# A decoder layer for Trainium2: stacked rows of the cross-attention scores laid 8 partitions apart, the queries' rounded parts sent from ScalarE's queue, and another merge order

## The reference

```
q = _w8a8_linear(x, wq, bq).reshape(B, N, H, D).transpose(0, 2, 1, 3)
k = (cond @ wk.T + bk).reshape(B, L, H, D).transpose(0, 2, 1, 3)
scores = jnp.einsum('bhnd,bhld->bhnl', q, k) * inv_sqrt_d + mask[:, None]
attn = jax.nn.softmax(scores, axis=-1)
```

## Time and profile before

| what | value |
|---|---|
| median of 3 runs | 423.77 us (422.56 to 424.12) |
| the profiled execution | 420.01 us, of which the span of the instructions is 418.2 us |
| PE busy | 365.5 us, 87% of the span |
| DVE busy | 293.8 us, 70% |
| ACT busy | 194.2 us, 46% |
| POOL busy | 149.2 us, 36% |
| TensorE's granted clock, mean | 0.935 of full speed |

### The profile page before, as it was taken

One profiled execution on the slowest core, in us unless ns is written; L12 is line 12 of the kernel. 1 busy time (PEld: TensorE's weight loads), 2 busy tenths in 40 slices (PEclk: granted clock), 3 DMA queues, 4 the chain that ended last, 5 costly groups with the idle time before them and its releaser, 6 DMA issues. The chain is left out here.

```text
span 418.2 us, 7505 instructions
## 1 busy us (share of the span) xinstructions
PE 365.5 (87%) x2526; PEld 309.2 (74%) x2526; DVE 293.8 (70%) x848; ACT 194.2 (46%) x352; POOL 149.2 (36%) x162
## 2 busy tenths in 40 slices
PE   8977879996899999997999999999998455887795
PEld 7646769884788888795898778979778435745684
DVE  3999957584687879965688479659857844775522
ACT  1573547152447664643738535456663020383230
POOL 5495738842633443424135234242223300000101
PEclk9998969998999999999999999999999955968889
DMA  8937134786523535765134247462222253000000
GB/s 295 353 104 262 52 126 151 220 163 148 103 102 96 160 103 150 118 145 117 53 104 125 77 152 114 101 115 79 79 63 102 44 69 39 16 2 2 0 27 25
DMA packets 29798, 45.55 MB, mean 109 GB/s; under 512 B 3648, under 2 KB 20544, under 8 KB 29760
## 3 DMA queue, kind: packets, MB, share of 16 engines
q1 hardware_dynamic: 28944, 44.28, 40.4%
q10 hardware_dynamic: 816, 0.79, 0.8%
HBM read 26.31 MB, written 5.24 MB: 75 GB/s over the span
## 5 line engine op out<-in xcount | busy, mean ns | idle before, releaser
L1426 POOL TENSOR_TENSOR q_T<-q_T,rope_s 128x512 f32<-128x512 f32 x24 | 30.7, 1284 | 74.0 <-DMA rope_s<-rope_t 72.1
L1242 DVE CUSTOM_DVE_ANT_0 q_int<-bank,mask_s 128x256 bf16<-128x256 f32 x128 | 45.2, 416 | 15.9 <-PE bank L698 15.7
L1437 POOL TENSOR_TENSOR a_lo<-a_flat,a_hi 128x512 fp32r<-128x512 f32 x32 | 41.4, 1296 | 38.2 <-ACT a_flat L875 38.2
L618 PE MATMUL acc<-wo_s,a_hi 128*128 128x256 f32 x256 | 49.9, 294 | 0.8 <-POOL a_lo L1437 0.8
L586 PE MATMUL bank<-v_s,p_near 128*128 128x129 f32 x256 | 42.9, 279 | 4.1 <-POOL p_near L1444 3.8
L586 PEld LDWEIGHTS bank<-v_s,p_near 128*128 128x128 f32 x256 | 37.1, 194 | 11.6 <-issue 9.5
L1461 POOL TENSOR_TENSOR small<-small,half 128x2 f32<-128x2 f32 (+1 forms) x16 | 10.5, 656 | 94.2 <-DVE small L1132 94.1
L618 PEld LDWEIGHTS acc<-wo_s,a_hi 128*128 128x128 f32 x256 | 40.3, 193 | 3.1 <-POOL a_lo L1437 1.4
L915 ACT ACTIVATE p_near<-bank 128x512 f32<-128x512 f32 x32 | 19.1, 596 | 48.2 <-PE bank L563 34.9
L513 PE MATMUL bank<-x_hi,wqkv_hi 128*128 128x256 f32 x124 | 39.2, 316 | 0.0
L563 PE MATMUL bank<-q_T,k_T 128*128 128x512 f32 x64 | 34.7, 627 | 1.9 <-POOL q_T L1426 1.9
(11 more groups left out here) (167 smaller groups left out, 953.8 us busy)
## 6 DMA issues: line engine op xcount, KB each, us to landing
wo_s<-wo_parts SPq DMA_DIRECT2D x24, 512.0 KB, 3.5
rope_s<-rope_t SPq DMA_DIRECT2D x54, 128.0 KB, 2.3
wo_parts<-wo_s SPq DMA_DIRECT2D x8, 512.0 KB, 3.1
kS<-xo_T SPq DMA_DIRECT2D x24, 128.0 KB, 4.6
qS<-xo_T SPq DMA_DIRECT2D x24, 128.0 KB, 4.3
xs<-in_wo SPq DMA_DIRECT2D x8, 256.0 KB, 4.7
stage<-in_wqkv SPq DMA_DIRECT2D x2, 512.0 KB, 5.2
xp_T<-in_wqkv SPq DMA_DIRECT2D x2, 512.0 KB, 6.9
```

Source lines behind the costliest of these rows:

```text
L618: ins = mm(acc[:, t, :], a[x], wo_s[:, slot, w, m, :], start=(j == 0 and t == 0 and m == 0 and p == 0), stop=(j == PAIRS - 1 and m == 1 an ...
L1242: v.tensor_tensor_reduce(out=q_int[:, m, :], in0=bank("xscore", b, j, 0, t)[:, m * T:(m + 1) * T], in1=mask_s[:, t, :], scale=-1.0, scalar ...
L1426: g.tensor_tensor(dst, dst, (rope_s if b else rope_t)[:, n % 2], ALU.add).then_inc(sig["rotated", 0], 1)
L1437: g.tensor_tensor(a_lo[:, j % 2], a_flat[:, j % 2], a_hi[:, j % 2].bitcast(F32), ALU.subtract)\
```

## The change

Three things are changed together. First, the 16 rows that one DMA writes in `kS` or `qS` no longer follow each other: feature `d` of head `m` and part `part` goes to row `3 * m + part + 8 * d`, so that the rows of one DMA lie 8 partitions apart. The matmul of the scores runs over 126 rows instead of 96 and the shifted one over 128 instead of 98; unused rows hold zeros on the queries' side. Second, ACT issues the four DMAs of the queries' `part_hi` itself, right after it has written that part; SP sends only the two of `part_lo`, and still all six of the keys. `send_k` of the first item now waits until the stacked buffers are cleared. Third, `ORDER` is another string. All operations and all matmuls are the same in number.

```diff
-XROWS = 2 * 3 * XD
-XSHIFT = XROWS + 2
+XSTEP = 8
+XROWS = P - 2
+XSHIFT = P
...
+        def part_rows(m, part):
+            r0 = 3 * m + part
+            return slice(r0, r0 + XSTEP * (XD - 1) + 1, XSTEP)
...
             def send_k(b):
                 wait_for(sp, "k_lo", b, 1)
                 wait_filled(sp, "xprob", b - 1, XPAIRS - 1, 0, 1)
+                if b == 0:
+                    sp.wait_ge(cleared, 2)
                 for m in range(2):
                     for part, src in enumerate((part_hi, part_lo, part_hi)):
-                        r0 = 3 * XD * m + XD * part
-                        sp.dma_start(kS[r0:r0 + XD].bitcast(F32), src[:, m, :]).then_inc(k_in, 16)
+                        sp.dma_start(kS[part_rows(m, part)].bitcast(F32), src[:, m, :]).then_inc(k_in, 16)
...
             def send_q(b):
...
                 for m in range(2):
-                    for part, src in enumerate((part_hi, part_hi, part_lo)):
-                        r0 = 3 * XD * m + XD * part
-                        sp.dma_start(qS[r0:r0 + XD, :, m, :].bitcast(F32), src[:, m, :]).then_inc(q_in, 16)
+                    sp.dma_start(qS[part_rows(m, 2), :, m, :].bitcast(F32), part_lo[:, m, :]).then_inc(q_in, 16)
...
             def turn_q(b):
...
                                bias=bias_c[:, 0, m:m + 1]).then_inc(sig["q_hi", 0], 1)
+                for m in range(2):
+                    wait_for(act, "q_hi", b, m)
+                    for part in (0, 1):
+                        act.dma_start(qS[part_rows(m, part), :, m, :].bitcast(F32), part_hi[:, m, :]).then_inc(q_in, 16)
```

Of `ORDER`, one line of the five before and now:

```diff
-    "nnmxsrssxmmxxxrnmxxxmxsxmxmmmmxxxmxonsxxmxmxxxxxnsoxxommxxmxmmmmmxmmxmmxmcmxcxcxxnxnxnxxxonnxxxxnxxnxxxxx"
+    "romnmxsxxxmnnxxmxmxnsxxmmmxxxmxrnxxxmmmxsxxxmsxmnmoxxmmxxxnmxmmmmmoxmmmxmxcxxnxnccnxxxnxxonxxxxxnxnxxxxxx"
```

More of the change, by code:

```diff
@@ L135 @@
 ORDER = (
-    "rrrrrrrsrssrmsmmscmsmmrrmmsmrmmmrsscrmmmcmmsmmmmmmrsmmsmmmrcmmmcmcmmccmcmrmcmmrrcmmmsrscsmxrrmxsmxmmxrmmm"
-    "xssrrsxxsxmxmmsmxxxsxmmmxxsmmmrxxmsmxxmmmmrxmmrxmrxxxxxxrmmxxmmxmxsxsmmmxrmxmcsxsrmsxmmsmncxncmrsxnmmmxmm"
-    "xrrsmmmxsxxmsxnnxmxrnmmxsxmxsmmxrmmxmrxxxmrxrmxmnmxmxxxxxmmnoxxsxxxronxmsxmmxossccmmcxnsmmmsnxorxmrmnmmxn"
-    "nnmxsrssxmmxxxrnmxxxmxsxmxmmmmxxxmxonsxxmxmxxxxxnsoxxommxxmxmmmmmxmmxmmxmcmxcxcxxnxnxnxxxonnxxxxnxxnxxxxx"
-    "xxxxxxxxxxxxnxxxonnnnnononnnnnnonnnonooo")
+    "rrrrrmsmrrrmssrmmsrssmmmcmmsrsmmmmsrrmmmmmrmmmcsmcrmssmmrmmmmccmmmmmccmccmcmrrmcrrcmsmmrsmmsxrmsrxsmxmmmx"
+    "xmsrrsmxxmmxxsmsmxxxxmmrmxxsmmsmxxmxmmxsxrxxmxxxxxmrrxxmmxmxmxsmmmsxmrsxmmmrmmxcmrsxmmnsrxsmxnscxmcmxrsmr"
+    "mxmsxmmxmxnnnmxnmmxxxnrsmxxmmsmxmsxmxmxxrxmrxxxmmrxxrmxrsxxmxxnmxmoxsmxoxnmmmcsmcmsxrcmoxrmmnsxmsnxmxmssm"
+    "romnmxsxxxmnnxxmxmxnsxxmmmxxxmxrnxxxmmmxsxxxmsxmnmoxxmmxxxnmxmmmmmoxmmmxmxcxxnxnccnxxxnxxonxxxxxnxnxxxxxx"
+    "xxxxxxxxxxxoonxxxnnnnnonononnnonnnnonono")
 def work_streams():
```

## The result

The changed kernel takes 407.18 us in the median (406.53 to 408.52, 4 runs), the one before 423.16 us beside it (421.70 to 424.12, 4 runs): a ratio of 0.963, with a 95% interval of 0.959 to 0.967. That is 16.0 us less. I had forecast 7.5 us less, and a range that ended at 410.5. The direction was right, the size was not.

The account below looks back on a forecast made before the run. PE, busy 87% of the span, was taken to lose most waiting for scores until the queries' DMAs land. Terms -4.1 - 5.0 + 3.6 - 2.0 = -7.5 us gave a median of 416.3 us, range 410.5 to 423.0.

Parts of the forecast that it names:

- The sends' pace: Key and query sends with rows 8 apart: 2.3 us each to land, at the issues' pace of 0.65 us.
- The slower rival: Sends keep their pace of 1.03 us per DMA despite spread rows: +9.7 us, 433.5 us; chance 10%.
- The estimate in the prediction: Queries' sends at 27.2 GB/s per port: 0.6 us per DMA, making the last item's term -3.8 rather than -4.1.
- The last item, -4.1 us: Last item: its first scores start at about 345.8 instead of 349.92, and the end moves as much.
- Items 0 to 2, -5.0 us: First scores of items 0 to 2: all 5.0 us of PE's waits for them go.
- the sends are not sooner: Items 0 to 2: late keys delay the queries' rounding and sends, the 5.0 us stay: 421.3 us; no separate chance.
- ACT's time, +3.6 us: Items 0 to 2: twelve issues in ACT's queue cost between nothing and 7.2 us; the middle taken.
- Swaps beside the keys, -2.0 us: Item 0: faster key sends shorten PE's 3.8 us wait for `p_near`; taken between 0 and -3.8.
- I let the end move as much: From the last item's first scores on, both orders nearly the same, so the end moves by the same 4.1 us.
- its best case: More gain: ACT's issues hidden and the whole 3.8 us of `p_near` gone, -12.9 us, 410.9 us; chance 15%.

Follow-up runs that it names:

- e_rows: The kernel before with only the rows of each send 8 apart; old order, all sends from SP: 407.35 us, ratio 0.973.
- e_step2: As e_rows, but with the 16 rows of a part 2 apart instead of 8: 405.90 us, ratio 0.965.
- e_rows_act: As e_rows, with the change's four sends of the queries' rounded parts on ACT: 407.20 us, ratio 0.971.
- e_early: The kernel before with the new order only for the first 84 operations, up to item 0's norm; sends as before: 411.27 us, ratio 0.981.
- e_early_rows: The diffs of e_rows and e_early together on the kernel before, all sends from SP: 396.25 us, ratio 0.941.
- e_warm: The kernel before with 22 matmuls on constants, results unused, in two of PE's waits in the last item: 419.02 us, ratio 0.994.
- e_send_later_sp: The change with item 0's key sends moved behind `near` 1.1 in the order and all sends from SP: 402.06 us, ratio 0.950.
- e_order: The kernel before with the new order alone; rows and sending queue as before: 428.44 us, ratio 1.023.

## Why the prediction was wrong, point by point

**The sends' pace: right for the keys, too fast for the queries.** I took the swap's 2.3 us to landing and the issue's 0.65 us as pace. The keys have 2.5 us, and landings at the pace of the issues. The slower rival, that the sends keep 1.03 us, is refuted by e_rows and e_step2. But for the queries I let two queues issue 0.6 us apart each and every send land after 2.3 us, 4.95 us from rounding to the last landing. Where PE waited for that landing it was 7.3 us in item 0 (94.72 to 102.05), 7.35 in item 1 (170.33 to 177.68) and 6.2 in the last item (334.86 to 341.04). The estimate in the prediction from the Trainium skill's page "SBUF — State Buffer", section "Door 1: The DMA port swizzle", six landings over 3.0 us even from two queues, was the better one: in the last item they take 3.2 us.

**The last item, -4.1 us: nearly right.** In the timeline after (start, duration, idle before):

```profile
326.82 1.37 DVE L1172 TENSOR_SCALAR q_int<-q_tmp 128x512 bf16<-128x512 f32 x1
...
334.86 0.84 ACT L963 ACTIVATE xo_T<-bank,bias_c 128x256 fp32r<-128x256 f32 x2 [2.14 <-DMA kS<-xo_T]
...
340.02 0.18 DVE L1340 TENSOR_SCALAR keep<-marked 128x32 bf16<-128x32 f32 x1
...
340.35 0.37 PE L767 MATMUL bank<-identb_s,keep 128*128 128x128 bf16 x2 [2.85 <-DVE keep L1340]
341.04 2.04 PE L703 MATMUL bank<-kS,qS 126*128 126x256 f32 x8 [0.32 <-issue]
```

From the quantised tokens (326.82 + 1.37 = 328.19) it takes 6.7 us to ACT's rounding, which waits for the keys as I said (6.5 forecast), 12.0 to the mask (12.0 forecast), and 12.85 to the scores (12.3 forecast, 15.0 before). With the 1.5 us by which the norm no longer waits behind `scale2` (its sum starts at 320.89, right behind the statistics at 320.77), that is -3.6.

**Items 0 to 2, -5.0 us: failed.** I let the 5.1 us by which the queries land sooner pay for the cover that the order takes away. The waits are 0.62, 4.16 and 0 us, 4.8 against 5.1. In item 1 (timeline after):

```profile
170.33 0.84 ACT L963 ACTIVATE xo_T<-bank,bias_c 128x256 fp32r<-128x256 f32 x2 [3.54 <-DMA kS<-xo_T]
...
177.68 1.19 PE L703 MATMUL bank<-kS,qS 126*128 126x256 f32 x4 [4.16 <-DMA qS<-xo_T]
```

Two things are late there. Four swaps hold SP from 157.49 for 7.02 us, only then come the keys' sends (164.61), and ACT waits for them before it rounds the queries at 170.33, 2.7 us after PE has turned them (167.59). That is the rival "the sends are not sooner", to which I gave no chance of its own. And the burst takes 7.35 us instead of 4.95, its last send 4.9 us to land. The two delays, 2.7 and 2.4 us, are more than the 4.16 us wait. In the old order, e_rows, 2.4 us of the three waits are left, so the step holds there by half.

**ACT's time, +3.6 us: not measurable.** I had no row that priced it and took the middle of 0 and 7.2. Three pairs of kernels with and without ACT's sends (0.971 and 0.973, 0.944 and 0.941, 0.948 and 0.950) show neither a price nor a gain beyond their intervals; a fourth (0.963 and 0.971) left it open. In the last item, for which I had set no price, e_rows_act shows both: the scores' wait falls by 3.7 us, and the waits for `z_T` and the mask take 3.5 us of it back. The Trainium skill's page "DMA: Bandwidth & Descriptors", section "Issuing engines are not separate DMA queues", says that a second issuing engine saves only the time of issuing. The runs agree in so far as none of the four pairs shows a gain beyond its intervals.

**Swaps beside the keys, -2.0 us: the right place, the wrong sign.** PE's 3.8 us wait for `p_near` went (1.8 us for `p_far` are left), but the new order puts the key sends ahead of the last weight loads and the swaps on the same queue, and that cost 5.0 us at a new place. I looked at what the queue does now, and not at what each operation is moved past on it.

**Left out: the first 82 us, -8.6.** This is the step that failed most: the sum has no term for it, because I costed the order only at the three places near the sends and put the rest at nothing without a reason. PE's waits for `a_s` stood in the same list as those for the scores, 9.0 us in three waits, more than any term I priced. The waits give 6.4 of the 8.6 us; PE's busy time, at a clock of 1.00 instead of 0.94, is another 1.7 shorter. e_early, with this part of the order alone, has the first norm 9.5 us sooner.

**Left out: the clock, -4.2.** I wrote that from the first scores on "I let the end move as much". PE's busy time in that stretch fell from 54.40 to 48.82 us for nearly the same matmuls (324 and 322), at a clock of 0.93 instead of 0.82. The same stretch in the old order takes from 62.8 us (e_rows, 0.94) to 68.3 us (before, 0.82), and at the change's clock, 0.93, it takes 63.7 (e_early_rows). So the 4.2 us go with PE's clock and not with the new order, and the profile before is the slow end. What sets the clock stays open: the first five us explain little of it (0.50 in e_early_rows, which takes 63.7 us), and e_warm's matmuls are worth 0.6% of the kernel.

My range ended at 410.5 since even its best case was a sum of the terms near the sends; a part of the list of waits and the clock lay outside all cases. That the direction came out right is no merit of the sum: its largest term failed, and what it left out made the gain.

## What to carry to other kernels

When a change brings a new order, walk the whole list of waits against it, not only the places that the rest of the change touches: here the largest term and the largest loss were both elsewhere. On a queue in order, ask of each moved burst what it is moved past; six small sends in front of a megabyte of loads, with swaps behind both, made a wait of 5.0 us, and moving one letter gave 1.5% back. Measure the parts of a change apart and then together: two of them alone (0.973 and 0.981) made a product below the whole (0.963), a hint that a third part cost time, and the two together (0.941) showed it before any trace named the place. And take the same stretch from several profiles before you explain its length: the last one, with the same operations, moved from 62.8 to 68.3 us.

## What was unexpected of the hardware

A DMA of 128 KB into 16 neighbouring partitions took 4.4 us to land in a burst of six, into 16 partitions 2 apart 2.5 us and 8 apart 2.4 us: that one step of spacing is enough, I had not expected. Of PE's clock these runs show no simple rule. Behind the last item's wait it stayed at 0.50 for the first five us of scores before the change and was 0.73 after it, where PE had been busy for 2.32 and 6.67 of the ten us ahead. But in e_send_later_sp PE was busy for 6.23 of those ten us and the clock behind them was 0.51, and in e_order for 0.44 and it was 0.67. So in these runs how busy PE was just ahead doesn't tell the clock that it gets.
